# A 2048 x 2048 adapter layer on one core: from plain fp16-split products to Strassen's seven block products on pairs of rows, in two passes

## The reference

```python
y = einsum('bct,bcd->bdt', x, w_cond[itok])            # 128x128 per row, over tokens
result = einsum('bnd,od->bno', y, W_base) + b_base     # 2048 x 2048, the bulk of the work
logits = einsum('bnd,ed->bne', y, W_gate)              # 8 experts
route_w = top-2 of softmax(logits), renormalised
h = einsum('bnd,erd->bner', y, A)                      # rank 16 per expert
delta = einsum('bner,eor->bno', h * route_w, B)
out = x + result + delta * (16 / R)
```

## Time and profile before

| | us |
|---|---|
| median of 3 runs (1685.47 to 1686.7) | 1686.07 |
| the profiled execution's own time | 1686.61 |
| its span, first to last instruction | 1684.7 |
| PE busy / DVE busy / ACT busy / POOL busy | 1645.8 / 827.8 / 247.7 / 223.6 |
| mean granted TensorE clock | 0.992 of full speed |

### The profile page before, as it was taken

How to read it: one execution, slowest core, us unless ns; L and a number is a source line. 1 busy time by engine, 2 the same in 40 slices (tenths; PEclk the granted TensorE clock), 3 DMA queues, 4 the chain that set the end, 5 groups by cost and what they waited for, 6 DMA issues and landing times.

```text
span 1684.7 us, 27043 instructions
## 1 busy us (share of the span) xinstructions
PE 1645.8 (98%) x10563; PEld 893.3 (53%) x10563; DVE 827.8 (49%) x1801; ACT 247.7 (15%) x416; POOL 223.6 (13%) x132
## 2 busy tenths in 40 slices
PE   5899999999999999999999999999999999999998
PEld 5785555455555455555545555554555554555553
DVE  5866554444545454454445444545445444544452
ACT  5661111001011101011110101110001111010110
POOL 2652111100111110111111011111011111101110
PEclk8999999999999999999999999999999999999999
DMA  6341110111110111111011111101111101111100
GB/s 228 126 177 59 46 52 19 51 45 45 51 45 28 42 51 45 45 45 51 24 46 45 45 51 45 39 31 51 45 45 51 45 25 45 45 51 45 45 25 25
DMA packets 32111, 89.49 MB, mean 53 GB/s; under 512 B 3386, under 2 KB 8506, under 8 KB 25946
## 3 DMA queue, kind: packets, MB, share of 16 engines
q1 hardware_dynamic: 32090, 89.21, 14.5%
HBM read 55.64 MB, written 33.55 MB: 53 GB/s over the span
## 4 chain that ended last, share of the span: by engine, by line
PE 95%; DVE 2%; issue 1%; ACT 1%; DMA 0%; SPq 0%; DVEq 0%; POOL 0%; ACTq 0%; POOLq 0%
PE acc L732 26%; PE acc L731 26%; PE acc L733 26%; PE h_ps L733 2%; PE h_ps L731 2%; PE h_ps L732 2%; PE tr L731 2%; PE delta L731 2%; PE tr L732 2%; PE tr L733 2%; PE delta L733 2%; PE delta L732 2%; PE tr L784 1%; DVE WT L504 0%; DMA x_even<-in_x_dram 0%
## 5 line engine op out<-in xcount | busy, mean ns | idle before, releaser
L732 PE MATMUL acc<-WT,y_parts 128*128 128x512 f16 (+2 forms) x2240 | 799.6, 361 | 0.0
L731 PE MATMUL acc<-WT,y_parts 128*128 128x512 f16 (+2 forms) x2240 | 799.3, 361 | 0.0
L733 PE MATMUL acc<-WT,y_parts 128*128 128x512 f16 (+2 forms) x2240 | 799.3, 361 | 0.0
L733 PEld LDWEIGHTS acc<-WT,y_parts 128*128 128x128 f16 x2240 | 219.8, 98 | 234.1
L731 PEld LDWEIGHTS acc<-WT,y_parts 128*128 128x128 f16 x2240 | 219.8, 98 | 219.1
L732 PEld LDWEIGHTS acc<-WT,y_parts 128*128 128x128 f16 x2240 | 219.8, 98 | 217.8
L504 DVE SCALAR_TENSOR_TENSOR y_parts<-tr,y_parts 128x512 f16<-128x512 f32 x126 | 86.9, 691 | 238.3 <-ACT y_parts L352 237.7
L592 DVE SCALAR_TENSOR_TENSOR scaled_acc<-acc,y_inv,inv_w 128x512 f32<-128x512 f32 x128 | 95.8, 749 | 189.2 <-PE delta L733 182.8
L352 ACT ACTIVATE y_parts<-tr 128x512 f16<-128x512 f32 x126 | 75.1, 597 | 502.0 <-PE tr L733 501.9
L299 POOL TENSOR_TENSOR wait_taker<-amax,ident 128x2 f32<-128x2 f32 x32 | 6.3, 197 | 947.4 <-DVE amax L483 947.4
L476 DVE TENSOR_SCALAR clamped<-amax_all 128x2 f32<-128x2 f32 x32 | 5.4, 170 | 210.9 <-POOL amax_all L300 210.9
(11 more groups left out here) (175 smaller groups left out, 1393.5 us busy)
## 6 DMA issues: line engine op xcount, KB each, us to landing
x_even<-in_x_dram SPq DMA_DIRECT2D x16, 1024.0 KB, 4.8
x_odd<-in_x_dram SPq DMA_DIRECT2D x16, 1024.0 KB, 4.8
out_dram<-x_even SPq DMA_DIRECT2D x64, 256.0 KB, 2.5
out_dram<-x_odd SPq DMA_DIRECT2D x64, 256.0 KB, 2.5
x_odd<-in_L_ffn_W_base_dram SPq DMA_DIRECT2D x4, 1024.0 KB, 5.0
bias<-in_L_ffn_W_base_dram SPq DMA_DIRECT2D x4, 1024.0 KB, 4.8
spare<-in_L_ffn_W_base_dram SPq DMA_DIRECT2D x4, 1024.0 KB, 4.9
x_parts<-in_L_ffn_W_base_dram SPq DMA_DIRECT2D x3, 1024.0 KB, 4.7
```

Of the source, the lines that this page charges most:

```text
L731: nc.tensor.matmul(dst, lhs[0], rhs[0], start=start, stop=False)
L732: nc.tensor.matmul(dst, lhs[0], rhs[1], start=False, stop=False)
L733: return nc.tensor.matmul(dst, lhs[1], rhs[0], start=False, stop=stop)
```

## The change

**The products.** Two batch rows are taken together as the two row blocks of a 2 x 2 block product. The features are halved, and the 2048 outputs are handled as two halves `s`, each of two blocks of 512. A step `n` takes one pair of rows and one half of the features: for each `s` it makes seven products of sums of blocks (4 k-chunks, 12 matmuls of 512 columns each) where a plain block product makes eight. 16 steps (the first pass, features 0 to 1023) write partial results to a scratch tensor in DRAM, then the second half of W_base is prepared, and 16 more steps (the second pass) add the rest, the features from DRAM, the routing and the delta products.

**What the other engines do instead.** ACT copies y out of PSUM, writes the upper parts of seven operands S, and copies four products out of PSUM to SBUF for each `s` (`copy_p`). DVE makes the sums and lower parts of S. A finished tile is one PSUM bank plus or minus one copy, times `inv_w`, plus the residual, three DVE instructions (`finish`). In the first pass POOL adds the bias to each residual tile of 512 (`add_bias`), eight times a step; in the second pass DVE adds eight delta tiles a step (`add_delta`). SP loads and stores the residual tile by tile through six buffers. W_base is prepared in 16 groups of 256 rows x 1024 features; each needs seven operands T (three blocks, four sums), and POOL makes the lower parts of the four sums. The eight groups of the second half stand between the two passes on all engines.

The core of the diff (the launch and the small buffers are left out):

```diff
+            def add_bias(m):
+                _, o = tile_of(m % 8)
+                pool.wait_ge(xr_in[xr_slot(m)], xr_turn(m))
+                nc.gpsimd.tensor_tensor(XR[:, xr_slot(m), :], XR[:, xr_slot(m), :], bias[:, o:o + Q],
+                                        ALU.add).then_inc(bias_added, 1)
...
+            for n in range(NSTEP):
+                if n + 1 < NSTEP:
+                    share_maxima(n + 1)
+                if n < NP:
+                    for j in range(8):
+                        add_bias(8 * n + j)
+                if n == NP - 1:
+                    for g in range(NU, 2 * NU):
+                        w_lower(g)
...
+            def w_upper(g):
...
+                act.wait_ge(w_tr, 4 * g + 1)
+                if g > 0:
+                    act.wait_ge(w_sum, 4 * g - 2)
+                nc.scalar.activation(c12, ring[4 * u % 5][:, :], ACT.Copy).then_inc(w_first, 1)
+                for i, q in ((1, B11), (2, B22), (3, B21)):
+                    act.wait_ge(w_tr, 4 * g + i + 1)
+                    nc.scalar.activation(t_dst(q, u, 0), quads(ring[(4 * u + i) % 5][:, :]), ACT.Copy).then_inc(w_first, 1)
+                for i, q in enumerate((T1, T3, T2, T4)):
+                    act.wait_ge(w_sum, 4 * g + i + 1)
+                    nc.scalar.activation(t_dst(q, u, 0), quads(t_full[q]), ACT.Copy).then_inc(w_sum_hi, 1)
...
+            def scale_x(n):
+                dve.wait_ge(amax_shared, n + 1)
+                power_of_two(pow2[:, :], amax_all[:, :], clamped[:, :])
+                link(nc.vector.reciprocal(rpow2[:, :], pow2[:, :]))
+                nc.vector.tensor_scalar(xw_scale[:, :], rpow2[:, :], TOP_X, None, ALU.mult).then_inc(x_scaled, 1)
+                nc.vector.tensor_tensor(X[:, 1, 0:Q], X[:, 1, 0:Q], X[:, 1, Q:KH], ALU.add).then_inc(xs_added, 1)
...
+            def finish(n, s, c):
...
+                nc.vector.scalar_tensor_tensor(out=TM[:, m % 2, :], in0=src[:, :],
+                                               scalar=y_inv[:, n % 2, c // 2:c // 2 + 1],
+                                               in1=PC[:, at, :], op0=ALU.mult, op1=op).then_inc(t_done, 1)
+                dve.wait_ge(t_done, m + 1)
+                nc.vector.tensor_tensor(TM[:, m % 2, :], TM[:, m % 2, :], inv_w[:, o:o + Q],
+                                        ALU.mult).then_inc(r_ready, 1)
+                dve.wait_ge(r_ready, m + 1)
+                if n < NP:
+                    dve.wait_ge(bias_added, m + 1)
...
+                nc.vector.tensor_tensor(XR[:, xr_slot(m), :], XR[:, xr_slot(m), :], TM[:, m % 2, :],
+                                        ALU.add).then_inc(r_added, 1)
...
+            for n in range(NSTEP):
+                more, second = n + 1 < NSTEP, n >= NP
+                if more:
+                    find_maxima(n + 1)
+                features(n)
+                if second:
+                    route_tokens(n)
+                    weigh_features(n)
+                finish(n, 0, C11)
+                if more:
+                    scale_x(n + 1)
+                if second:
+                    split_hwT_lo(n)
+                if more:
+                    split_x_lo(n + 1, 0)
+                    split_x_lo(n + 1, 1)
+                finish(n, 0, C12)
...
+                finish(n, 1, C21)
+                finish(n, 1, C22)
...
+            def cond(n, u):
+                i, half = ((0, 0), (1, 0), (0, 1), (1, 1))[u]
+                pe.wait_ge(xp_lo, 2 * n + 1 + i)
...
+                product(n, 0, 0)
+                make_features(n)
+                for q in range(1, NPROD):
+                    product(n, 0, q)
+                    if q == 4 and second:
+                        transpose_hw(n)
+                    if q == 5 and more:
+                        cond(n + 1, U_A11)
+                    if q == 6:
+                        if more:
+                            cond(n + 1, U_S1)
+                        if second:
+                            delta(n, 0)
+                for q in range(NPROD):
+                    product(n, 1, q)
+                    if q < 2 and more:
+                        cond(n + 1, (U_A12, U_A22)[q])
+                    if second and q < 6:
+                        delta(n, q + 1)
+                        if q == 5:
+                            delta(n, 7)
```

More of the change, by code:

```diff
@@ L9 @@
 O = 2048
-KC = T // P
-OC = 512
-NOC = O // OC
+NP = NB // 2
+KH = T // 2
+C4 = 4
+Q = C4 * P
+NSTEP = 2 * NP
 E, R = 8, 16
@@ new lines, in adaln_ffn_kernel, with n_copy, n_tile, n_s @@
+        P1_COPY, P5_COPY, U2_COPY, P4_COPY = range(4)
+        def n_copy(n, s, i):
+            return 4 * (2 * n + s) + i + 1
+        C11, C12, C21, C22 = range(4)
+        def n_tile(n, s, c):
+            return 4 * (2 * n + s) + c + 1
+        def n_s(n, q):
+            return NPROD * n + q + 1
+        def xr_slot(m):
+            return m % NXR
+        def xr_turn(m):
+            return 16 * (m // NXR + 1)
+        def tile_of(j):
+            s, c = j // 4, j % 4
+            return c // 2, s * KH + (c % 2) * Q
@@ new lines, in copy_p @@
+            def copy_p(n, s, i):
+                par = n % 2
+                src, q, at, row = ((BX[s], 0, 0, 0), (BY[1], 1, 1, 1), (BX[s], 3, 0, 0), (BZ, 4, 2, 1))[i]
+                act.wait_ge(prod_done, n_prod(n, s, q))
+                before = 2 * n + s - 1
+                if i == P1_COPY and before >= 0:
+                    act.wait_ge(t_done, n_tile(before // 2, before % 2, C12))
+                elif i == U2_COPY:
+                    act.wait_ge(t_done, n_tile(n, s, C11))
+                elif i == P5_COPY and before >= 0:
+                    act.wait_ge(t_done, n_tile(before // 2, before % 2, C22))
+                elif i == P4_COPY and before >= 0:
+                    act.wait_ge(t_done, n_tile(before // 2, before % 2, C21))
+                nc.scalar.activation(PC[:, at, :], src[:, :], ACT.Copy,
+                                     scale=y_inv[:, par, row:row + 1]).then_inc(p_copied, 1)
@@ new lines, in product @@
+            def product(n, s, q):
+                before = 2 * n + s - 1
+                if s == 0:
+                    pe.wait_ge(s_lo, n_s(n, q))
+                if q == 0 and n > 0:
+                    pe.wait_ge(t_done, n_tile(n - 1, s, C22))
+                elif q == 1 and before >= 0:
+                    pe.wait_ge(t_done, n_tile(before // 2, before % 2, C12))
+                elif q == 2 and before >= 0:
+                    pe.wait_ge(t_done, n_tile(before // 2, before % 2, C11))
+                elif q == 3:
+                    pe.wait_ge(p_copied, n_copy(n, s, P1_COPY))
+                elif q == 4 and before >= 0:
+                    pe.wait_ge(p_copied, n_copy(before // 2, before % 2, P4_COPY))
+                elif q == 5:
+                    pe.wait_ge(p_copied, n_copy(n, s, P5_COPY))
+                elif q == 6:
+                    pe.wait_ge(p_copied, n_copy(n, s, U2_COPY))
+                dst = (BX[s], BY[1], BY[0], BX[s], BZ, BY[1], BX[s])[q]
+                opens = q in (0, 1, 2, 4)
+                for c in range(C4):
+                    mm = three(dst[:, :], [SO[:, slot(n, q), part, c, :] for part in range(2)],
+                               [TT[:, q, s, part, c, :] for part in range(2)],
+                               opens and c == 0, c == C4 - 1, q not in (2, 4))
+                mm.then_inc(prod_done, 1)
```

1479 lines of the change are left out of this document (829 added, 650 removed).

## The result

The changed kernel takes 1892.33 us (median of 4 runs, 1887.37 to 1895.75), the kernel before 1686.38 us beside it (4 runs, 1685.47 to 1688.86). The ratio is 1.1216 with a 95% interval of 1.1182 to 1.125: 12% slower. Its profiled span is 1886.9 us. The forecast was 1773 us with a range of 1690 to 1812, so slower was right and the size was not.

What follows compares the result with a forecast made beforehand. Before, PE's matmuls bound the kernel. 110 start + 16 x 49.1 + 79 switch + 16 x 50.0 = 1774.6, less 4.3 and 5.5, plus 6.8: span 1771.6, forecast 1773 us, range 1690 to 1812.

Steps and rivals of the forecast that it cites:

- What bounds before, and what PE is spared: Old kernel bound by PE's matmuls, 49.66 us a row; new steps without waits 41.8 and 47.2 us, 165 us less.
- the chain of the first pass: First-pass step, shared maximum through bias, C11 and scales to split x at 24.0 us: PE waits 5.7, step 49.1.
- POOL's burst stops 128x4: First-pass scales: DVE's 128x4 instructions alternate with POOL's five biases, about 1.2 us of POOL before each.
- POOL stops less: Rival, first-pass scales: 128x4 runs beside POOL, only C11's add is held; 1691 to 1750 us, middle 1716; chance 0.17.
- The clock: Behind PE's 5.7 us wait in each first-pass step, a lower granted clock costs 1.6 us.
- Behind 2.8 us I add nothing: Second-pass wait of PE: no clock loss counted; if the clock falls there too, 26 us for the pass.
- The second pass: C11, scales, ACT, then DVE's lower half at 21.3 us; PE waits 2.8 us, a step of 50.0 instead of 47.2.
- The start: Preparing the first half of W_base and first operands before the first product: 110 us, bounds 80 and 125.
- The switch: Between the passes, last tiles and eight more weight groups with PE nearly idle: 79 us, bounds 62 and 95.
- faster: Rival: x is split before PE's first cond asks, before 20.5 and 21 us; 1601 to 1682 us, chance 0.17.
- 6.53 us of sharing: First pass, from the end of DVE's maxima to POOL's shared maximum: 6.53 us that no order of DVE's shortens.

Runs made afterwards that it cites:

- e1: The changed kernel with POOL adding the bias of three tiles ahead of the next step's shared maximum, five behind it: 1670.05 us, ratio 0.9909.
- e9: e6 plus maxima over tiles found one step earlier and, on ACT, the upper part of x ahead of the bank_x copy: 1644.12 us, ratio 0.9749.
- e3: The changed kernel with POOL's maximum over the partitions replaced by a copy of each partition's own maximum: 1656.38 us, ratio 0.9828.
- e2: The changed kernel with seven of POOL's eight biases held back until the next step's x is split: 1822.93 us, ratio 1.0817.
- e4: The changed kernel with 48 unread matmuls added ahead of the first cond in each first-pass step: 1856.03 us, ratio 1.1013.
- e5: e1 plus, in the second pass, DVE making the next step's scales ahead of tile C11's tail: 1697.71 us, ratio 1.0068.
- e10: e1 plus the first step's shared maximum put behind the weights' second part on POOL, not the fourth: 1664.07 us, ratio 0.9871.
- e6: e5 plus the first step's shared maximum put behind the weights' second part on POOL, not the fourth: 1681.24 us, ratio 0.9979.

## Why the prediction was wrong

- **What bounds before, and what PE is spared**: right. I had 41.8 and 47.2 us for a step without waits; e1's first pass and e9's second show 42.0 and 47.4.
- **The step that failed** is in the chain of the first pass: "Only then does POOL begin the bias of this step's tiles, and tile C11 [...] waits for it: 1.27 us each [...], so 14.95". I let the bias start 0.1 us behind the reduction. It starts 7.06 us behind it, since POOL stands idle between the two, a term that my sum did not have. From `amax_shared` to `w_cond_parts` I had 24.0 - 13.6 = 10.4 us and the timeline shows 547.85 - 531.05 = 16.8; these 6.4 (6.96 for the bias, less 0.6 by which the rest of the chain came out shorter) and half a microsecond of clock are the 6.8 of the step. e1 and e3 remove the wait from two sides.
- The kernel before could have told me: its show a bias with 6.71 us of idle time, which I read past since the releaser named was DVE, and its view of waits has the same gap without a releaser in 25 steps:

```profile
POOL x_even L303 <- issue: 91.3, 13, 7.3
POOL x_odd L303 <- issue: 85.4, 12, 7.6
```

  There the bias waited for `xw_parts` at about the same time, so it cost nothing. The change put something in front of it that needs the bias, and the cover was gone.
- **POOL's burst stops 128x4**: right, in kind and size. I took 1.2 us for each POOL instruction ahead of a DVE one; shown are 1.67, 1.22, 1.18 and 0.97. e2 prices it at 4.1 us a step. The rival "POOL stops less" is out. The Trainium skill's SBUF — State Buffer, Who interferes with whom, has a tensor_scalar able to take the ports that DVE shares with GpSimd, and an add with two SBUF inputs contend with GpSimd's reads. These rows agree with both; the reciprocal between them, which that section does not name, ran in 0.18 us.
- **The clock**: mis-sized a little. I had 1.6 us behind a wait; e4 shows 2.1 behind one of 12 us. And "Behind 2.8 us I add nothing" held by luck, since the wait came out at 1.86, behind which the clock fell once in the second pass (at 1.94); e5 has it falling behind 13 of 14 waits of 2.10 to 2.16.
- **The second pass**: right. C11 to the scales to ACT to DVE ran as worked out; the wait was 1.86 us for 2.8.
- **The start**: mis-sized by 19 us. The switch was 8 us shorter than I had it. For the start, two causes are seen. ACT stood 8.82 us (74.4 to 83.23) for scales whose maxima DVE had ready at 49.3, since POOL did the reduction behind the weights' fourth part: 7.1 us by e10. POOL made `ident` only at 11.22 us and ACT waited 5.1 us for its neighbour `ones`. The rest was not tried.
- **The rival "faster"** named the right condition: `xp_lo` before 20.5 and 21 us. The 6.53 us of sharing which I set against it were not the obstacle; e1 has them still and meets the condition in both passes: counted from a step's first product, its first cond starts at 19.5 us or earlier in the first pass and at 20.7 or earlier in the second. In e9 it is 18.4 and 18.8 to 18.9, about where PE arrives by itself (18.4 and 18.6).

## What to carry to other kernels

Before an operation is put behind another of a different kind on the same engine, look in the trace for idle time without a releaser between such a pair, even where it costs nothing today: the change may take its cover away. A reorder on one engine's queue has to be carried through every queue of the chain, or the wait only moves, and near 2 us a few tenths of waiting went with a lower clock for what followed (e1 and e5).

## What the runs showed of the hardware

- GpSimd took 5.84 us from an ordinary instruction to `partition_all_reduce` and 7.06 us back (0.39 us of work between); without the reduction (e3) both are gone. The trace has a pair of MODIFY_POOL_CONFIG for each way: one pair under L411 ahead of each reduction, and one under the line of the next instruction, in the first pass L423, right behind it (531.01 us in the step above):

```profile
L411 POOLq MODIFY_POOL_CONFIG  x64: 8/11/11, 76.4 to 1793.3; - x64
L411 POOL PARTITION_ALL_REDUCE amax_all<-amax x32: 385/386/388, 82.0 to 1799.0; - x32
```

```profile
L423 POOLq MODIFY_POOL_CONFIG  x32: 82/83/83, 141.1 to 980.0; - x32
```

  The Trainium skill's GPSIMD Engine Reference, Instruction dispatch, says that the first call to freshly loaded code, measured from a MODIFY_POOL_CONFIG, pays about 6 us which no instruction of the profile shows. The trace agrees for the way in (5.84) and has 1.1 us more for the way back. Read as holding for both ways, that rule would have put the return into the forecast's sum.
- The changed kernel's first affine select on GpSimd started at 11.22 us with 10.29 us of idle time and no releaser, in the kernel before at 1.41. In e3, without the reduction, it started at 1.19. Why the kernel before, which has the reduction, was spared is open.
- At the same place of the program the granted clock stayed at 1.00 behind the 1.87 us without matmuls of e1, and fell to 0.50 behind 13 of the 14 waits of 2.10 to 2.16 us of e5. That is not a limit: it stayed at 1.00 behind 2.12 (e6) and fell behind 1.94 (changed kernel). A fall cost 1.7 us there, and 2.1 behind 12 us (e4).
